# Softmax sums of 16 heads taken from ones in the unused value columns, in place of eight separate matmuls per batch

## The chip, the cores and the metric

The kernel runs on one core of one Trainium2 chip. The metric is the device time of one execution in microseconds (us), lower is better. Engines are TensorE (PE, with its weight loads shown apart as PEld), VectorE (DVE), ScalarE (ACT), GpSimd (POOL) and SyncE (SP), which issues most transfers. All data is fp32.

## What is computed

Four transformer blocks run one after the other on x (16 batches of 128 rows of 256) with a context of the same shape. The change concerns the attention with 16 heads of width 16, which occurs in block 0 (self attention, then cross attention), in block 1 (ten chosen rows of each batch) and in block 3 (cross attention). Cut to what matters:

```python
def _mha(q_in, kv_in, in_w, in_b, out_w, out_b):
    q, k, v = heads(...), heads(...), heads(...)          # (16 batches, 16 heads, 128 rows, 16)
    scores = jnp.einsum('bhqd,bhkd->bhqk', q, k) / jnp.sqrt(jnp.float32(dh))
    attn = jax.nn.softmax(scores, axis=-1)
    out = jnp.einsum('bhqk,bhkd->bhqd', attn, v)
    out = out.transpose(0, 2, 1, 3).reshape(q_in.shape[0], q_in.shape[1], D)
    return out @ out_w.T + out_b

x = x + _mha(_ln(x), _ln(x), ...)          # block 0, first stage
x = x + _mha(_ln(x), _ln(ctx), ...)        # block 0, second stage; then a mixture of 8 experts, 2 per row
x = ... ten rows of each batch replaced by their attention to ctx      # block 1
x = ... grouped attention with 4 key heads and a gated MLP             # block 2, not touched
x = x + _mha(layer_norm(x), ctx, ...)      # block 3
```

## The kernel before, in words

`attention` (L526) is a pipeline over batches, called twice: with two stages (32 batches, block 0, with the router of the experts mixed in from slot 20 on) and with one stage (16 batches, block 3). Each engine runs one Python loop over a slot number t, so what an engine does in slot t stands in the order in which the loop writes it, and semaphores tie the engines together. Where a text speaks of the start of slot t, it is the start of that slot's `scores_turned` (L679). In a slot of the middle:

- PE: `scores(t + 1)` (L669) writes the scores of the next batch to four PSUM banks `scores`; then work for the groups ahead (turns L645, projections L652, value projections L661); `products(t - 1)` (L689 and L694) into PSUM bank 4; more work for the groups ahead; `scores_turned(t)` (L679), which writes the same four banks; a turn of the row maxima (L811); and, in odd slots, `rows_out` (L704), the output projection of two finished batches.
- DVE: the row maxima of batch t + 1 (L1006, two instructions over 128x1024); in even slots the addition of the output rows to x (L1022); the division for batch t - 1 (L1027, L1028); the maxima subtracted in the queries (L1038); statistics of the batch 11 ahead (L983 to L990).
- ACT: copies and projections' biases (L839 to L867), then the exponentials of batch t (L912, two instructions), whose results are the turned probabilities `PT2`.
- POOL: standardizes the rows of the groups of four batches ahead (L944) and adds the output bias to x (L951).

The four banks `scores` are written twice in a slot, so a slot has a loop through three engines: L679 writes them, L912 reads them, L669 writes them, L1006 reads them, and the next L679 may start.

A slot's work ahead depends on its phase, (t + 5) % 4. Phase 0 (t = 3, 7, ...) has two turns of 4 x 128 columns, as has phase 1 in the two stages that attend to the context; phase 1 in the self attention and phase 2 there have one projection of 512 columns ahead of `scores_turned`; phase 2 in the other stages and phase 3 have two pieces of that kind, or a projection and values. The additions L1022 come in phases 1 and 3.

Values are kept padded (`VP`, and `tok_V` in block 1): each head has 32 columns, of which 16 hold its values and 16 hold zeros, values first for even heads and last for odd ones. Two heads thus add up to the 32 rows of bank 4 that belong to r, and four r run in four column tiles of PE. Columns 0 to 255 of bank 4 get the numerators, columns 256 to 511 the sums, from a stationary operand `ones_half` that is one in half its columns. DVE then takes the reciprocal of 128x256 sums and multiplies. Block 1 does the same for groups of four batches in `products` (L1909 on), `divide` (L2151 on) with `tok_` names; its four groups g = 0 to 3 are handled in a loop of their own.

## Time and profile before

| what | value |
|---|---|
| median of 3 runs | 1432.4 us (1427.1 to 1432.89) |
| profiled execution: span from first to last instruction | 1426.0 us |
| profiled execution: PE busy | 1293.6 us, 91% of the span |
| DVE / ACT / POOL busy | 673.4 / 622.1 / 429.4 us |
| first call of `attention` (slots 0 to 31) | about 35 to 340 us of the span |
| block 1 | about 700 to 810 us |
| second call of `attention` (slots 0 to 15) | about 1278 to 1423 us |

The profile describes one execution. What the execution takes outside its span is not in it: the median of the runs is 6.4 us above the span, the lowest run 1.1 us. A row of the timeline gives the start and length of a few merged instructions, the engine, the line, the instruction, and in brackets the idle time ahead with the instruction that ended it. Matmuls in fp32 appear as two records each, so the 16 matmuls of `products` are x32.

### The profile page before, as it was taken

Reading aid. Unit: us, or ns where it says so; the run is one execution under the profiler, and the core shown is the slowest. Engines: PE = TensorE matmul, PEld = TensorE weight load, DVE = VectorE, ACT = ScalarE, POOL = GpSimd, SP = SyncE. Lnnn points to the kernel's source line nnn. Section 1 sums busy time; section 2 is a strip of 40 time slices with the busy share of each in tenths; the row PEclk is TensorE's granted clock in tenths of the full one; section 3 lists DMA queues with packets and bytes.
Section 4 is the critical chain, followed back from the end, with each engine's and each line's share of the span. In section 5 each row is a group of like instructions: output and inputs, shape, how many; then the busy total and the mean of one; then the engine's idle time right before and its main releaser. Section 6 shows DMA issues by size and latency. Waiting matters only on the chain. (4 is left out here: it accounts for less than half of the span.)

```text
span 1426.0 us, 34137 instructions
## 1 busy us (share of the span) xinstructions
PE 1293.6 (91%) x13946; PEld 1054.6 (74%) x13946; DVE 673.4 (47%) x1457; ACT 622.1 (44%) x1444; POOL 429.4 (30%) x549
## 2 busy tenths in 40 slices
PE   4899999976799999999688899999999998859996
PEld 2566666655589999998576678888888887736665
DVE  3676777677322000000654645546446445146666
ACT  2444445521445544444222255545546546135442
POOL 3224446153323222244100143433423423032200
PEclk9999999987799999999666999999999999979998
DMA  9000000000589999996410000000000000000000
GB/s 298 2 2 2 2 2 15 11 17 24 133 291 335 344 344 351 355 352 221 148 32 2 3 1 2 2 1 2 1 2 1 2 2 1 1 1 2 17 17 31
DMA packets 80042, 120.11 MB, mean 84 GB/s; under 512 B 12112, under 2 KB 62544, under 8 KB 79760
## 3 DMA queue, kind: packets, MB, share of 16 engines
q1 hardware_dynamic: 73840, 106.62, 22.4%
q0 software_dynamic: 4768, 10.26, 2.0%
q8 instruction: 112, 1.84, 0.6%
q10 hardware_dynamic: 1280, 1.04, 0.2%
q14 instruction: 42, 0.34, 0.1%
HBM read 108.43 MB, written 9.48 MB: 83 GB/s over the span
## 5 line engine op out<-in xcount | busy, mean ns | idle before, releaser
L1759 ACT ACTIVATE w_ca<-scores,fc1b 128x128 f32<-128x128 f32 x312 | 114.5, 368 | 139.7 <-PE scores L1714 118.6
L912 ACT ACTIVATE reg<-scores 128x1024 f32<-128x1024 f32 x96 | 93.1, 1021 | 160.9 <-PE scores L679 160.7
L1714 PEld LDWEIGHTS scores<-reg 128*128 128x128 f32 x1248 | 146.7, 194 | 6.4 <-issue 2.5
L1714 PE MATMUL scores<-reg 128*128 128x128 f32 x1248 | 147.7, 277 | 3.1 <-issue 1.1
L1724 PE MATMUL bank<-reg,w_ca 128*128 128x256 f32 x624 | 141.1, 379 | 0.3 <-DVE small L1784 0.3
L1006 DVE TENSOR_REDUCE reg<-scores 128x8 f32<-128x1024 f32 x96 | 113.0, 1219 | 54.6 <-PE scores L669 54.5
L2311 ACT ACTIVATE reg<-reg,mx 128x128 f32<-128x128 f32 x256 | 99.1, 389 | 85.1 <-DVE mx L2460 84.8
L2386 POOL TENSOR_TENSOR reg<-reg,rden 128x512 f32<-128x512 f32 x64 | 66.6, 1041 | 212.3 <-DVE rden L2465 212.2
L1793 DVE TENSOR_TENSOR reg<-bank,reg 128x256 f32<-128x256 f32 x39 | 16.6, 425 | 240.9 <-PE bank L1724 232.7
L1724 PEld LDWEIGHTS bank<-reg,w_ca 128*128 128x128 f32 x624 | 115.6, 190 | 14.5 <-DVE small L1784 0.3
L1576 PE MATMUL scores<-reg 128*128 128x128 f32 x1024 | 122.5, 279 | 0.5 <-ACT reg L2327 0.5
L1576 PEld LDWEIGHTS scores<-reg 128*128 128x128 f32 x1024 | 119.8, 196 | 0.7 <-ACT reg L2327 0.7
L2248 PE MATMUL bank<-reg,w_ca 128*128 128x256 f32 x512 | 118.8, 385 | 0.8 <-issue 0.8
L2248 PEld LDWEIGHTS bank<-reg,w_ca 128*128 128x128 f32 x512 | 94.7, 190 | 26.6 <-issue 13.2
L1027 DVE RECIPROCAL reg<-bank 128x256 f32<-128x256 f32 x48 | 84.2, 1754 | 30.6 <-PE bank L694 29.8
L852 ACT ACTIVATE reg<-bank,qk_bias,shape_c 128x512 f32<-128x512 f32 x96 | 69.6, 779 | 59.1 <-PE bank L652 58.8
L1141 POOL DMA_INDIRECT expert_out<-reg,block_ids_of x39 | 39.5, 1012 | 143.1 <-DVE reg L1793 75.0
L2471 DVE TENSOR_TENSOR w_ca<-scores,w_ca 128x512 f32<-128x512 f32 x32 | 22.1, 692 | 109.9 <-PE scores L1576 109.9
L679 PEld LDWEIGHTS scores<-reg 32*128 32x128 f32 x1536 | 48.3, 189 | 31.8 <-issue 31.7
L669 PEld LDWEIGHTS scores<-reg 32*128 32x128 f32 x1536 | 50.0, 193 | 28.7 <-ACT reg L912 20.2
L679 PE MATMUL scores<-reg 32*128 32x128 f32 x1536 | 57.2, 286 | 14.0 <-DVE reg L1006 14.0
L669 PE MATMUL scores<-reg 32*128 32x128 f32 x1536 | 59.5, 291 | 7.8 <-ACT reg L912 5.1
(278 smaller groups left out, 2347.5 us busy)
## 6 DMA issues: line engine op xcount, KB each, us to landing
reg<-in_fc SPq DMA_DIRECT2D x78, 1024.0 KB, 7.4
reg<-expert_out SPq DMA_DIRECT2D x16, 256.0 KB, 3.9
xres<-in_x SPq DMA_DIRECT2D x4, 512.0 KB, 10.6
ctxr<-in_ctx SPq DMA_DIRECT2D x1, 2048.0 KB, 14.8
w_l<-in_w_l SPq DMA_DIRECT2D x2, 1024.0 KB, 12.1
routed_rows<-reg SPq DMA_DIRECT2D x8, 256.0 KB
out<-xres SPq DMA_DIRECT2D x8, 256.0 KB, 2.6
w_sa<-in_w_sa SPq DMA_DIRECT2D x1, 1024.0 KB, 8.5
```

The costliest lines, as they stand in the source:

```text
L669: ins = nc.tensor.matmul(S[r][:, (2 * s + c) * P:(2 * s + c + 1) * P], Qs[rows_of(r), (b // GB) % 2, s, c, batch(b)], Ks[rows_of(r), (b // ...
L679: ins = nc.tensor.matmul(S[r][:, (2 * s + c) * P:(2 * s + c + 1) * P], Ks[rows_of(r), (b // GB) % 2, s, c, batch(b)], Qs[rows_of(r), (b // ...
L852: ins = nc.scalar.activation(dst[:, g % 2, s, m, :], bank[:, :], ACT.Identity, scale=scale[:, s:s + 1], bias=bias[:, s, m:m + 1])
L912: ins = nc.scalar.activation(PT2[:, t % 2, 2 * half:2 * half + 2, :, :, :].rearrange("p r s c q -> p (r s c q)"), scores4[:, 2 * half:2 * ...
L1006: ins = nc.vector.tensor_reduce(mxpad.rearrange("p (c n d) -> p n c d", c=C, d=DH)[:, 4 * half:4 * half + 4, :, 0], scores4[:, 2 * half:2 ...
L1027: link(nc.vector.reciprocal(rd, banks[4][:, 2 * P:4 * P]))
L1576: ins = nc.tensor.matmul(bank[:, k * P:(k + 1) * P], w[:, c, w0:w0 + P], src[:, c, :], start=(c == 0), stop=(c == C - 1))
L1714: ins = nc.tensor.matmul(S[n % 4][:, 0:P], up_w8[j % 2][:, c, f * P:(f + 1) * P], xbT[:, j % 2, c, :], start=(c == 0), stop=(c == C - 1))
L1724: ins = nc.tensor.matmul(T[j % 2][:, 0:D], h1[:, j % 2, f, :], down_w8[j % 2][:, f, :], start=(f == 0), stop=(f == FC - 1))
L1759: nc.scalar.activation(h1[:, j % 2, f, :], S[n % 4][:, 0:P], ACT.Gelu, bias=fc1b[:, bass.ds(e * FC + f, 1)]).then_inc(M["fc1_free"], 1)
L2248: ins = nc.tensor.matmul(bank[:, 0:D], src[:, f, :], w[:, f, :], start=(f == 0), stop=(f == FC - 1))
L2311: ins = nc.scalar.activation(v[:, a, :], v[:, a, :], ACT.Exp, bias=cols_of(mx, n)[:, a:a + 1], accum_out=cols_of(psum, n)[:, a:a + 1])
```

## The change

Values are padded with ones in place of zeros. One matmul of a head then gives 32 rows: 16 of numerators and 16 copies of the head's sum. The heads no longer add up in pairs: even heads go to columns 0 to 255 of bank 4, odd heads to columns 256 to 511, each matmul starting and ending its own accumulation. The eight `ones_half` matmuls of a batch go, and the 16 of `products` stay (in block 1, 64 stay and 8 go per group).

Numerator and sum of a head now stand in different rows. DVE turns bank 4 in blocks of 32x32 (128x512, from PSUM), takes the reciprocal of one of each 16 equal sums (128x16 in all), and turns these, spread over 16 columns each, back into rows (128x256), so that each numerator has its inverse sum beside it. ACT copies the even half of bank 4, with the rows that hold sums scaled to zero; DVE adds the odd half, likewise masked, and multiplies with the inverse sums. A batch has three more DVE instructions and one more ACT instruction, and four fresh waits. PE may overwrite bank 4 when the masked sum is made (`nd_read`), no longer after the multiplication (`o_ok`).

The diff also drops functions that nothing calls (`Jobs`, `dve_softmax`, `pe_products` and others), and four memsets of `ones_half` at the start. Its core:

```diff
+        def inverse_sums(dve, link, turned, out_, sums_read, k):
+
+            nc.vector.transpose(turned, banks[4][:, :]).then_inc(sums_read, 1)
+            dve.wait_ge(sums_read, k)
+            sums_of = turned[:, DH:DH + 2 * (C * P - DH)].rearrange("p (u x) -> p u x", u=2)[:, :, 0:C * P - DH:32]
+            link(nc.vector.reciprocal(den_inv[:, :, :].rearrange("p n u -> p u n"), sums_of))
+            link(nc.vector.transpose(out_.rearrange("p (n u d) -> p n u d", n=8, u=2),
+                                     den_inv[:, :, :].unsqueeze(3).to_broadcast([P, 8, 2, DH])))
...
                     def products(b):
-                        for c in range(C):
-                            for s in range(2):
+                        for odd in range(2):
+                            for c in range(C):
                                 for r in range(4):
-                                    nc.tensor.matmul(banks[4][rows_of(r), c * P:(c + 1) * P],
-                                                     VP[:, (b // GB) % 2, b % GB, 8 * c + 2 * r + 1 - s, :],
-                                                     PT2[:, b % 2, r, s, c, :], start=(s == 0), stop=(s == 1))
-                        for s in range(2):
-                            for r in range(4):
-                                ins = nc.tensor.matmul(banks[4][rows_of(r), C * P:2 * C * P], ones_half[:, s, :],
-                                                       PT2[:, b % 2, r, s, :, :], start=(s == 0), stop=(s == 1))
+                                    a0 = (2 * odd + c) * P
+                                    ins = nc.tensor.matmul(banks[4][rows_of(r), a0:a0 + P],
+                                                           VP[:, (b // GB) % 2, b % GB, 8 * c + 2 * r + odd, :],
+                                                           PT2[:, b % 2, r, 1 - odd, c, :], start=True, stop=True)
                         ins.then_inc(M["nd_full"], 1)
...
                             if t - 1 >= 1:
-                                pe.wait_ge(M["o_ok"], t - 1)
+                                pe.wait_ge(M["nd_read"], t - 1)
...
                         if t < LATE:
                             routed_rows(t)
+                        if 0 <= t - 1 < N:
+                            act.wait_ge(M["sums_read"], t)
+                            if t - 1 >= 1:
+                                act.wait_ge(M["nd_read"], t - 1)
+                            nc.scalar.activation(even_part, banks[4][:, 0:2 * P], ACT.Copy, scale=head_rows[:, 1:2])\
+                                .then_inc(M["num_ok"], 1)
                         if 0 <= t < N:
                             act.wait_ge(M["st_full"], t + 1)
...
                             dve.wait_ge(M["nd_full"], b + 1)
-                            link(nc.vector.reciprocal(rd, banks[4][:, 2 * P:4 * P]))
-                            nc.vector.tensor_tensor(oT_a[:, (b // 2) % 2, :, (b % 2) * P:(b % 2 + 1) * P],
-                                                    banks[4][:, 0:2 * P].rearrange("p (c q) -> p c q", c=C),
-                                                    rd.rearrange("p (c q) -> p c q", c=C), ALU.mult).then_inc(M["o_ok"], 1)
+                            inverse_sums(dve, link, den_turned, rd, M["sums_read"], b + 1)
+                            dve.wait_ge(M["num_ok"], b + 1)
+                            o = oT_a[:, (b // 2) % 2, :, (b % 2) * P:(b % 2 + 1) * P]
+                            nc.vector.scalar_tensor_tensor(out=o, in0=banks[4][:, 2 * P:4 * P].rearrange("p (c q) -> p c q", c=C),
+                                                           scalar=head_rows[:, 0:1], in1=even_part.rearrange("p (c q) -> p c q", c=C),
+                                                           op0=ALU.mult, op1=ALU.add).then_inc(M["nd_read"], 1)
+                            dve.wait_ge(M["nd_read"], b + 1)
+                            nc.vector.tensor_tensor(o, o, rd.rearrange("p (c q) -> p c q", c=C), ALU.mult).then_inc(M["o_ok"], 1)
...
-                            nc.vector.memset(VP[:, 0, :, :, :], 0.0).then_inc(M["pad_ok"], 1)
-                            nc.vector.memset(VP[:, 1, :, :, :], 0.0).then_inc(M["pad_ok"], 1)
+                            nc.vector.memset(VP[:, 0, :, :, :], 1.0).then_inc(M["pad_ok"], 1)
+                            nc.vector.memset(VP[:, 1, :, :, :], 1.0).then_inc(M["pad_ok"], 1)
...
+                def even_heads(g):
+                    act.wait_ge(M["tok_sums_read"], g + 1)
+                    if g > 0:
+                        act.wait_ge(M["tok_nd_read"], g)
+                    nc.scalar.activation(tok_even, banks[4][:, 0:2 * P], ACT.Copy, scale=head_rows[:, 1:2])\
+                        .then_inc(M["tok_num_ok"], 1)
...
+                    even_heads(g)
                     if g + 1 < G:
                         queries(g + 1)
```

Block 1 has the same edits in its `products` and `divide`, with `tok_` names.

PE in slot 4 of block 0's first stage, before: a projection, `products`, the eight matmuls with `ones_half`, then `scores_turned`.

```order
L652 MATMUL bank<-reg,w_sa 128x512 [waits b_free,a_free,sub_ok]
L652 MATMUL bank<-reg,w_sa 128x512
L689 MATMUL bank<-reg 32x128 [waits o_ok,p_ok]
L689 MATMUL bank<-reg 32x128 x15
L694 MATMUL bank<-reg,ones_half 32x256 x8
L679 MATMUL scores<-reg 128x128 [waits max_ok,sub_ok]
L679 MATMUL scores<-reg 128x128 x15
```

The same place after the change:

```order
L474 MATMUL bank<-reg,w_sa 128x512 [waits b_free,a_free,sub_ok]
L474 MATMUL bank<-reg,w_sa 128x512
L512 MATMUL bank<-reg 32x128 [waits nd_read,p_ok]
L512 MATMUL bank<-reg 32x128 x15
L501 MATMUL scores<-reg 128x128 [waits max_ok,sub_ok]
L501 MATMUL scores<-reg 128x128 x15
```

The row with `ones_half` is gone, and `products` waits for `nd_read` in place of `o_ok`; nothing else on PE moves.

DVE in slot 4, before, from the maxima to the subtraction:

```order
L1006 TENSOR_REDUCE reg<-scores 128x4x2 [waits s_full]
L1006 TENSOR_REDUCE reg<-scores 128x4x2
L1022 TENSOR_TENSOR xres<-bank,xres 128x512 [waits biased,c_full]
L1027 RECIPROCAL reg<-bank 128x256 [waits nd_full]
L1028 TENSOR_TENSOR reg<-bank,reg 128x2x128 [waits chain]
L1038 SCALAR_TENSOR_TENSOR reg<-bank,shape_c,reg 128x2x128 [waits mt_full]
```

And after:

```order
L831 TENSOR_REDUCE reg<-scores 128x4x2 [waits s_full]
L831 TENSOR_REDUCE reg<-scores 128x4x2
L847 TENSOR_TENSOR xres<-bank,xres 128x512 [waits biased,c_full]
L341 STREAM_TRANSPOSE reg<-bank 128x512 [waits nd_full]
L344 RECIPROCAL den_inv<-reg 128x2x8 [waits sums_read]
L345 STREAM_TRANSPOSE reg<-den_inv 128x256 [waits chain]
L855 SCALAR_TENSOR_TENSOR reg<-bank,shape_c,reg 128x2x128 [waits num_ok,chain]
L859 TENSOR_TENSOR reg<-reg 128x2x128 [waits nd_read]
L867 SCALAR_TENSOR_TENSOR reg<-bank,shape_c,reg 128x2x128 [waits mt_full]
```

Five instructions, each waiting for the one ahead of it or for ACT, stand where two stood.

ACT in slot 4, before: the biases of a projection, then the exponentials.

```order
L839 ACTIVATE reg<-bank,cols 128x512 [waits b_full]
L852 ACTIVATE reg<-bank,qk_bias,shape_c 128x512 [waits a_full]
L852 ACTIVATE reg<-bank,qk_bias,shape_c 128x512
L912 ACTIVATE reg<-scores 128x1024 [waits st_full]
L912 ACTIVATE reg<-scores 128x1024
```

And after:

```order
L658 ACTIVATE reg<-bank,cols 128x512 [waits b_full]
L671 ACTIVATE reg<-bank,qk_bias,shape_c 128x512 [waits a_full]
L671 ACTIVATE reg<-bank,qk_bias,shape_c 128x512
L732 ACTIVATE reg<-bank,shape_c 128x256 [waits nd_read,sums_read]
L737 ACTIVATE reg<-scores 128x1024 [waits st_full]
L737 ACTIVATE reg<-scores 128x1024
```

The copy of the even heads (L732) stands in ACT's queue ahead of the exponentials, and waits for DVE's first block turn (`sums_read`).

## Rows read from the trace of the kernel before

**Rows 1.** The page: busy time of the engines over the span.

```profile
PE 1293.6 (91%) x13946; PEld 1054.6 (74%) x13946; DVE 673.4 (47%) x1457; ACT 622.1 (44%) x1444; POOL 429.4 (30%) x549
```

**Rows 2.** Waits of PE, whole span: engine, line, waited for; us in total, times, longest.

```profile
PE scores L679 <- DVE reg L1006: 14.0, 10, 3.4
```

**Rows 3.** Timeline of slot 4, block 0: start us, us, engine, line.

```profile
76.15 1.98 PE L652 MATMUL bank<-reg,w_sa 128*128 128x512 f32 x4
76.29 2.36 DVE L1006 TENSOR_REDUCE reg<-scores 128x8 f32<-128x1024 f32 x2 [1.37 <-PE scores L669]
...
78.07 1.08 PE L689 MATMUL bank<-reg 128*32 128x128 f32 x32
...
78.56 0.68 DVE L1022 TENSOR_TENSOR xres<-bank,xres 128x512 f32<-128x512 f32 x1
...
78.97 1.05 PE L694 MATMUL bank<-reg,ones_half 128*32 128x256 f32 x16
...
79.94 1.17 PE L679 MATMUL scores<-reg 32*128 32x128 f32 x32
80.08 1.76 DVE L1027 RECIPROCAL reg<-bank 128x256 f32<-128x256 f32 x1 [0.83 <-PE bank L694]
...
81.18 1.94 ACT L912 ACTIVATE reg<-scores 128x1024 f32<-128x1024 f32 x2 [1.56 <-PE scores L679]
```

**Rows 4.** Timeline of slot 12, block 3 (no work ahead left).

```profile
1384.65 1.17 PE L679 MATMUL scores<-reg 32*128 32x128 f32 x32 [0.69 <-DVE reg L1006]
...
1391.38 0.68 DVE L1022 TENSOR_TENSOR xres<-bank,xres 128x512 f32<-128x512 f32 x1
1391.61 1.17 PE L679 MATMUL scores<-reg 32*128 32x128 f32 x32 [0.70 <-DVE reg L1006]
...
1392.84 1.94 ACT L912 ACTIVATE reg<-scores 128x1024 f32<-128x1024 f32 x2 [5.03 <-PE scores L679]
```

**Rows 5.** Timeline: starts of slots 2, 3, 11 and 12, block 0.

```profile
64.34 1.17 PE L679 MATMUL scores<-reg 32*128 32x128 f32 x32
...
71.82 1.17 PE L679 MATMUL scores<-reg 32*128 32x128 f32 x32
...
143.03 1.17 PE L679 MATMUL scores<-reg 32*128 32x128 f32 x32
...
150.42 1.17 PE L679 MATMUL scores<-reg 32*128 32x128 f32 x32
```

**Rows 6.** Timeline of slots 9 and 10, block 0, where DVE waits for POOL.

```profile
125.63 4.85 POOL L944 TENSOR_SCALAR reg<-ctxr,mv,rstd 128x256 f32<-128x256 f32 x4
...
130.57 0.43 DVE L983 BATCH_NORM_STATS2 st<-xres 128x6 f32<-128x256 f32 x1 [5.59 <-issue]
...
133.99 1.17 PE L679 MATMUL scores<-reg 32*128 32x128 f32 x32 [2.04 <-DVE reg L1006]
...
135.37 3.58 PE L661 MATMUL bank<-w_sa,reg 128*128 128x256 f32 x8
```

**Rows 7.** Timeline of group 0, block 1.

```profile
720.61 1.91 PE L1926 MATMUL bank<-w_sa,ones_half 128*32 128x256 f32 x16
...
725.02 1.10 PE L1934 MATMUL bank<-w_l,reg 128*128 128x256 f32 x4 [1.41 <-DVE reg L2154]
```

**Rows 8.** Groups of instructions by line and form: busy us, mean ns, idle before.

```profile
L1027 DVE RECIPROCAL reg<-bank 128x256 f32<-128x256 f32 x48 | 84.2, 1754 | 30.6 <-PE bank L694 29.8
...
L694 PE MATMUL bank<-reg,ones_half 128*32 128x256 f32 x768 | 51.6, 387 | 0.0
...
L1038 DVE SCALAR_TENSOR_TENSOR reg<-bank,shape_c,reg 128x256 f32<-128x256 f32 x96 | 41.8, 477 | 25.8 <-PE bank L811 22.0 <-remote 3.7
...
L1022 DVE TENSOR_TENSOR xres<-bank,xres 128x512 f32<-128x512 f32 x24 | 16.4, 683 | 4.5 <-PE bank L704 4.4
...
L2465 DVE RECIPROCAL rden<-psum 128x4 f32<-128x4 f32 x64 | 11.2, 175 | 7.7 <-ACT reg L2311 6.9
...
L2327 ACT ACTIVATE reg<-scores 128x256 f32<-128x256 f32 x16 | 6.1, 381 | 10.0 <-PE scores L2255 10.0
```

More of the change, by code:

```diff
@@ L50 @@
 ROWS = ["sa_ob", "ca_ob", "l1_ob", "l3_ob", "l1_sw"]
-class Jobs:
-    def __init__(self, names):
-        self.at = {n: (k % 2, k // 2) for k, n in enumerate(names)}
-        assert len(self.at) == len(names)
-    def __getitem__(self, name):
-        return self.at[name]
 def build(nc, A, out):
@@ L358, in pe_turn_rows @@
-        def pe_turn_rows(pe, J, names, src, ok):
-            for c in range(C):
-                bank = claim(pe, J, names[c])
-                for j in range(GB):
-                    if c == 0 and ok is not None:
-                        pe.wait_ge(ok, j + 1)
-                    ins = nc.tensor.transpose(bank[:, j * P:(j + 1) * P], src[:, j, c * P:(c + 1) * P], ident[:])
-                ins.then_inc(q_full[J[names[c]][0]], 1)
-        def act_affine(act, J, names, dst, gain, bias):
-            for c in range(C):
-                bank = await_full(act, J, names[c])
-                if gain is None:
-                    ins = nc.scalar.activation(dst[:, c, :], bank[:, :], ACT.Copy)
-                else:
-                    ins = nc.scalar.activation(dst[:, c, :], bank[:, :], ACT.Identity, scale=col(gain, c),
-                                               bias=col(bias, c) if bias else 0.0)
-                ins.then_inc(q_free[J[names[c]][0]], 1)
@@ L495, in act_products @@
-        def act_products(act, J, name, bv, dst_cols):
-            bank = await_full(act, J, name)
-            for c in range(C):
-                ins = nc.scalar.activation(oT[:, c, dst_cols], bank[:, c * P:(c + 1) * P], ACT.Identity, bias=col(bv, c))
-            ins.then_inc(q_free[J[name][0]], 1)
         class Home:
```

155 lines of the change are left out of this document (23 added, 132 removed).

## The prediction, made before the changed kernel ran

> **What bounds the kernel now.** I read the page's busy shares first, then who PE waits for, then the timeline of single slots, which decides. PE is busy for 91% of the span [rows 1], and its largest wait inside the two calls of `attention` is for the maxima, 14.0 us in ten waits [rows 2]. So these 48 slots are mostly a queue of PE work; but the loop through three engines lies close under it, and the price of anything taken off PE must be read against that loop.
>
> Slot 4 shows both [rows 3]. From `scores_turned` to the exponentials is 81.18 - 79.94 = 1.24 us, and they take 1.94; the next scores begin right behind, so this part of a slot is always about 3.23. The other part runs from L669 to the next L679. PE's queue fills it here: L652 at 76.15, `products` at 78.07, the sums at 78.97, L679 at 79.94. DVE's maxima began at 76.29 and ended by 78.56, 1.4 us before L679 started. Slot 12 of block 3 has no work ahead, and there the maxima end last: PE idles 0.70 before L679, and the slot takes 1391.61 - 1384.65 = 6.96 us [rows 4]. That is the floor, with or without the sums. Slots of phase 0 take 71.82 - 64.34 = 7.48, those of phase 1 with context 150.42 - 143.03 = 7.39 [rows 5]: they can lose 0.5 and no more.
>
> **What goes from PE.** Eight matmuls of 256 columns per batch, 51.6 us of busy time in 48 batches [rows 8], 1.05 us each with overlaps. What the queue gains is the distance: from the start of the sums to L679 is 79.94 - 78.97 = 0.97, and from the end of `products` (79.15) to that of the sums (80.02) 0.87 [rows 3]. I take 0.90. The 16 matmuls that stay have the same form; only their targets and flags change.
>
> **What DVE gets.** Before: reciprocal and product, 80.08 to 82.29 by slot 4's pattern, of which 1.754 is the reciprocal [rows 8] and about 0.42 the product. After: a block turn of 128x512 from PSUM, a reciprocal of 128x16, a block turn of 128x256, the masked sum, the product. The reciprocal costs (1754 - 175) / 252 = 6.27 ns per element by its two sizes [rows 8], so 16 elements cost 175 + 12 x 6.27 = 250 ns. The masked sum is the form of L1038, 0.48 us; the product as before, 0.42. No block turn is in this trace. Its lower bound is the plain pass over 128x512 from PSUM, 0.683 us (L1022), its upper bound the reciprocal's rate, 6.27 ns per element: 3.3 us, and 1.7 for the 256. I take 0.68 and 0.42, the pass, because a turn moves each element once and computes nothing, as L1022 nearly does. The sum is 0.68 + 0.25 + 0.42 + 0.48 + 0.42 = 2.25 us. Two instructions with no wait between them overlap by 0.09: the maxima last until 76.29 + 2.36 = 78.65, and L1022 starts at 78.56 [rows 3]. A wait costs that overlap and, I estimate, some 0.03 more. With three more waits DVE's part is about 2.3 instead of 2.15 from its start to that of the subtraction: 0.15 us longer per slot. DVE is at 47% [rows 1], but where it ends a slot, this counts.
>
> The Trainium skill (VectorE: DVE Perf Modes, section Rules for kernel authors) speaks against this change: for chained DVE operations it says to minimize the number of operations. By that rule five in place of two are a loss. In the rows the fixed share of an instruction is small against the reciprocal: even with three more instructions the sum is only 0.15 longer, so the rule changes nothing in the working beyond that. For the block turn, the Trainium skill (Vector Engine (DVE) Microarchitecture Reference, section The reshape front-end and per-opcode configuration) states one element per cycle and lane; no run here shows it yet, and with it the sum would be the one I use.
>
> **What ACT gets, and who waits.** The even half is 128x256 from PSUM: 0.381 us as L2327 [rows 8]. It stands ahead of the exponentials in ACT's queue and waits for the first block turn, which waits for `nd_full` and stands on DVE behind the maxima and, in even slots, behind L1022. So a second path leads to the exponentials: maxima end, L1022 (0.60), block turn (0.06 + 0.70), copy (0.05 + 0.38 + 0.05). From the end of the maxima this is 1.24 us without and 1.84 with L1022; the path over L679 is 0.14 + 1.24 = 1.38 (L679 starts 0.23 after L1022, which starts 0.09 before the maxima end) [rows 4]. Hence in slots where the maxima end last, an even slot's exponentials now come 0.46 later than L679 alone would let them; in phase 1 with context this eats the gain of 0.4 down to 0.1, since the exponentials could start no earlier than 0.1 before where they do now. `nd_read` comes several us before the next `products`, and `o_ok` a slot before its `rows_out`; both are covered by the slot itself.
>
> **The 48 slots**, by what ends last after the change:
> - PE's queue, with long work behind `products` or ahead of it (slots 1, 2, 5, 6, 21, 22, 25, 26 of block 0; 1, 2, 5, 6, 9, 10 of block 3): 14 x 0.90 = 12.6 us.
> - Phase 1 of the self attention and slots 23 and 24: in slot 4 the copy would end at 79.15 + 0.06 + 0.70 + 0.48 = 80.39, against 81.18 now: 4 x 0.8 = 3.2.
> - Phase 0 (five slots of block 0, two of block 3): down to the floor, 7 x 0.45 = 3.2.
> - Phase 1 with context: 5 x 0.1 = 0.5.
> - Three pairs, slots 9/10, 13/14 and 17/18. POOL standardizes until about 130.5, DVE's statistics wait for it for 5.59 us, the maxima stand behind them, and PE idles 2.04 [rows 6]. Those chains start from DVE statistics two slots earlier and hold no PE work, so nothing is gained, and DVE's longer part (0.15) and the copy behind L1022 (0.3) are lost: 3 x -0.45 = -1.4.
> - Slots 27 to 31 of block 0 (the router's work on DVE) and 11 to 15 of block 3: held by the maxima, even slots lose 0.3: -1.6.
> - Tails: the last `products`, divisions and projections, where PE, DVE and PE follow each other: +0.5 and +1.2.
> - The two first slots: nothing.
>
> Sum 12.6 + 3.2 + 3.2 + 0.5 - 1.4 - 1.6 + 1.7 = 18.2 us.
>
> **Block 1.** The four groups run at the lower clock (1.91 us for the sums) and `products`, division, L1934 follow each other directly: PE idles 1.41 before L1934 [rows 7]. Of 1.9 saved, the longer division takes 0.5 (0.15, and ACT's copy and queue): 3 x 1.3, and 0.5 in the last group, where the clock is up and other matmuls stand between: 4.4 us. Nothing else changes: the memsets write ones at the cost of zeros, the four POOL memsets at the start lie under the first loads.
>
> **Total** 22.6 us off the span of 1426.0. The median of the runs lies 6.4 above the span, the lowest 1.1; I set the saving against the median: 1432.4 - 22.6 = 1409.8.
>
> **Rivals.**
> - *The block turn takes twice a pass* (1.22 us for 512 elements, 0.68 for 256), for fp32 moved in two halves. Then the path over the copy is 0.54 longer. Twelve of the slots with long work do not see it; two and the four of the second group lose 0.54 each, seven of phase 0 0.42, five of phase 1 0.54, the pairs 1.3, ten at the ends 0.5, tails and block 1 0.8 six times: 3.2 + 2.9 + 2.7 + 3.9 + 5 + 4.8 = 22.5. That eats all: 1432. For it: nothing in the trace shows a turn. Against it: a pass needs no second read. 0.10.
> - *The clock.* PE idled 2.04 before slot 10, and the L661 behind it took 3.58 us where others take 1.9: 1.7 lost [rows 6]. The change makes idle time of what it saves: about 1.2 to 1.8 in slots 14 and 18, which have none now. Should the granted clock fall there too, and in two to four slots near the ends, 3.4 to 10 us go: 1413 to 1420. 0.14.
> - *The maxima are no floor*: if DVE picks up faster or the L679 queue moves up everywhere, 48 x 0.97 + 7 - 2 = 51, 1381. The 0.70 of idle time in rows 4 speaks against it. 0.04.
> - *Slower*: the block turn at half the reciprocal's rate, 3.4 ns per element: 1.75 and 0.88 us. The path over the copy grows by 1.07 and DVE's part by 1.5. Then the short slots lose 1.0 to 1.5 each: some 6 x 1.07 + 12 x 1.0 + 3 x 2.6 + 10 x 1.07 + 6 x 1.5 = 46, and the time is 1432.4 + 23 = 1456. It decides from about 2.4 ns per element, where the gain is nil. Nothing but the lack of a row speaks for it. 0.06.
> - The forecast, 1399 to 1418, has 0.66.
>
> **How the numbers follow.** Low end: 0.97 in place of 0.90 in 18 slots (1.3 more), floor slots losing 0.5 (0.3), block 1 at the full 1.9 each (3.2), and runs as near their span as the lowest one (5.3 below the median): 1399.7, so 1399. High end: the clock at its worst (1420) or turns half as dear again as a pass (half of 22.5 lost, 1421), and 3 for the runs' spread: 1424. A measurement of this kernel can tell about 0.5% from no change, 7 us. Faster by more than that: 0.66 + 0.14 + 0.04 = 0.84; within it 0.10; slower 0.06.
>
> **What would show it.** The page after should have PE busy about 55 us less (51.6 and block 1's 6.0, less some). Block turns in the groups of instructions at 0.68 and 0.42 us; the floor slots at 6.96 to 7.1; slot 4 at 7.3; the pairs unchanged at 20.1 to 20.3 us; PE's waits for the maxima up from 14 us to some 20. In the copy's row, idle time ended by the block turn. I am wrong if the turns cost over 1 us, if ACT's wait for them holds back the exponentials in slots of long work too, or if slots fall under 6.9.

## The result, and the profile after

| | before | after |
|---|---|---|
| median of the runs | 1432.41 us (1427.1 to 1432.89) | 1418.49 us (1415.44 to 1418.86) |
| ratio, 95% interval | | 0.990, 0.9876 to 0.9924 |
| span of the profiled execution | 1426.0 us | 1416.9 us |
| start of slot 0 to start of slot 27, block 0 | 246.49 us | 241.53 us |
| slot 27 to slot 31, block 0 | 37.37 us | 43.84 us |
| block 1, start to the first scores of block 2 | 117.2 us | 116.7 us |
| block 2, untouched by the change, to slot 0 of block 3 | 475.8 us | 473.1 us |
| slot 0 to slot 15, block 3 | 125.53 us | 119.93 us |

The kernel became 13.9 us faster, where 22.6 were forecast. The two profiled executions differ by 9.1 us only: that of before is one of its faster ones (its runs in all comparisons reach from 1423.8 to 1439.3 us), that of after lies at its median. Not all of the 9.1 is the change's, either: 2.7 us of it lie in block 2, whose code is the same (471.4 to 479.7 us in the other twelve profiled executions). One of the four executions of experiment nine's kernel was in a slower state of the chip (1575.9 us, granted clock 0.81) and is left out.

Page of after: busy time of the engines, the line that answers to [rows 1]. PE lost 29.6 us of busy time and not 55: what it lost in matmuls it partly gave back in slower ones. In slots 28 to 31, with fewer matmuls, it is busy for 35.8 us and not 29.1 (granted clock 0.62, 0.82 before), and in block 1 it is busy as long as before, 95.4 and 95.2 us (0.66, 0.71 before).

```profile
PE 1264.0 (89%) x13114; PEld 1044.7 (74%) x13114; DVE 681.5 (48%) x1613; ACT 644.4 (45%) x1496; POOL 430.3 (30%) x545
```

Groups of after by line and form (busy us, mean ns, idle before), which answer to [rows 2, 8]: PE's matmuls of `scores_turned` (L501), then the division on DVE (block turn L341, reciprocal L344, second block turn L345, masked sum L855, product L859) and ACT's copy of the even half (L732).

```profile
L501 PE MATMUL scores<-reg 32*128 32x128 f32 x1536 | 64.3, 308 | 32.6 <-DVE reg L831 31.6 <-issue 1.0
...
L341 DVE STREAM_TRANSPOSE reg<-bank 128x512 f32<-128x512 f32 x48 | 34.1, 711 | 11.2 <-PE bank L512 9.6 <-remote 1.4
L855 DVE SCALAR_TENSOR_TENSOR reg<-bank,shape_c,reg 128x256 f32<-128x256 f32 x48 | 23.2, 484 | 4.8 <-ACT reg L732 3.2
L345 DVE STREAM_TRANSPOSE reg<-den_inv 128x256 f32<-128x256 f32 x52 | 23.2, 445 | 1.8
L732 ACT ACTIVATE reg<-bank,shape_c 128x256 f32<-128x256 f32 x48 | 22.8, 474 | 104.3 <-DVE reg L341 104.3
L859 DVE TENSOR_TENSOR reg<-reg 128x256 f32<-128x256 f32 x48 | 22.1, 461 | 1.7
...
L344 DVE RECIPROCAL den_inv<-reg 128x16 f32<-128x16 f32 x48 | 12.2, 254 | 1.6
```

The division is 0.711 + 0.254 + 0.445 + 0.484 + 0.461 = 2.36 us, where 2.25 was worked out: each part came out 0.004 to 0.04 dearer. But the wait of PE for the maxima rose from 14.0 to 31.6 us and not to 20, and the mean of the L501 matmuls from 286 to 308 ns: stretches at the lower clock that were not there before. The timeline of slots 9 and 10 of after shows both; it answers to [rows 6].

```profile
119.23 4.85 POOL L769 TENSOR_SCALAR reg<-ctxr,mv,rstd 128x256 f32<-128x256 f32 x4
...
124.17 0.43 DVE L808 BATCH_NORM_STATS2 st<-xres 128x6 f32<-128x256 f32 x1 [6.66 <-issue]
...
127.59 2.09 PE L501 MATMUL scores<-reg 32*128 32x128 f32 x32 [4.25 <-DVE reg L831]
129.61 0.69 PE L630 MATMUL bank<-ident,reg 128*128 128x128 f32 x2
130.09 3.57 PE L483 MATMUL bank<-w_sa,reg 128*128 128x256 f32 x8
```

By the kernel's semaphores, DVE's statistics of a group's first batch (L808) write a buffer that POOL reads until the end of its standardization (the trace names no releaser, but they start 0.09 us after it), and the maxima stand behind them. PE came to the wait sooner, so it waited 4.25 us instead of 2.04, and the scores behind took 2.09 us instead of 1.17: slot 10 takes 13.51 us (12.16 before) and slot 11 9.75 (9.04). The hold has a length of its own: from POOL's first instruction for the group to the start of slot 10, 14 or 18 it is 16.11 us in all three places before, and 16.36 to 16.40 after. Before, PE's own queue was just as long in slots 14 and 18, so that it showed no wait there; after, it waits. Slot 18 before, then after:

```profile
203.52 1.99 PE L661 MATMUL bank<-w_ca,reg 128*128 128x256 f32 x8
205.45 1.17 PE L679 MATMUL scores<-reg 32*128 32x128 f32 x32
```

```profile
197.19 0.43 DVE L808 BATCH_NORM_STATS2 st<-xres 128x6 f32<-128x256 f32 x1 [5.72 <-issue]
...
200.62 1.17 PE L501 MATMUL scores<-reg 32*128 32x128 f32 x32 [2.35 <-DVE reg L831]
```

### The profile page after: what moved, and what is told of

Read it like the earlier page. It is cut to its first block and busy times, and to the rows that moved or that the text cites. A ratio compares the mean times of both kernels' runs of the same rounds, so it can differ in the third digit from the quotient of the medians.

```text
span 1416.9 us, 32778 instructions
## 1 busy us (share of the span) xinstructions
PE 1264.0 (89%) x13114; PEld 1044.7 (74%) x13114; DVE 681.5 (48%) x1613; ACT 644.4 (45%) x1496; POOL 430.3 (30%) x545
## 5 line engine op out<-in xcount | busy, mean ns | idle before, releaser
L501 PE MATMUL scores<-reg 32*128 32x128 f32 x1536 | 64.3, 308 | 32.6 <-DVE reg L831 31.6
L501 PEld LDWEIGHTS scores<-reg 32*128 32x128 f32 x1536 | 54.9, 208 | 48.8 <-issue 48.7
L491 PEld LDWEIGHTS scores<-reg 32*128 32x128 f32 x1536 | 50.0, 192 | 29.8 <-ACT reg L737 21.4
L732 ACT ACTIVATE reg<-bank,shape_c 128x256 f32<-128x256 f32 x48 | 22.8, 474 | 104.3 <-DVE reg L341 104.3
L491 PE MATMUL scores<-reg 32*128 32x128 f32 x1536 | 59.7, 290 | 8.8 <-ACT reg L737 6.6
```

What stands on the lines that cost most here:

```text
L491: ins = nc.tensor.matmul(S[r][:, (2 * s + c) * P:(2 * s + c + 1) * P], Qs[rows_of(r), (b // GB) % 2, s, c, batch(b)], Ks[rows_of(r), (b // ...
L501: ins = nc.tensor.matmul(S[r][:, (2 * s + c) * P:(2 * s + c + 1) * P], Ks[rows_of(r), (b // GB) % 2, s, c, batch(b)], Qs[rows_of(r), (b // ...
```

## The experiments

Each ran against the kernel before, in four comparisons; with that of the result they are five, in which the median of before moved between 1431.2 and 1434.6 us. So two experiments of different comparisons are held against each other by their ratios; their medians alone can be off by 3 us. Slot lengths are of one profiled execution each. "Slot n" is the time from the start of that slot's `scores_turned` back to that of the slot before it.

### The two halves of the change apart

**One.** In the kernel before, the sums' matmuls are taken out, in every batch but the first of each call and in block 1, and nothing else. The division then works on old sums: this kernel leaves out what makes its result right, and only its time is of use.

```diff
-                        for s in range(2):
-                            for r in range(4):
-                                ins = nc.tensor.matmul(banks[4][rows_of(r), C * P:2 * C * P], ones_half[:, s, :],
+                        if b == 0:
+                            for s in range(2):
+                                for r in range(4):
+                                    ins = nc.tensor.matmul(banks[4][rows_of(r), C * P:2 * C * P], ones_half[:, s, :],
```

> The kernel before, with its eight matmuls on ones_half left out in every batch but the first of each call, and in block 1 altogether, so that the division works on old sums; DVE and ACT do exactly what they did. This is what PE gains, alone. Theory A (the clock): block 0 gets ahead by some 6 to 8 us until slot 27, then PE's longer idle time there lets the granted clock fall, and block 0 ends within 3 us of the kernel before; the whole is 10 to 16 us faster, 1417 to 1422. Theory B (the longer division and ACT's wait take the gain back): here they are absent, so block 0 ends 12 us or more earlier, and the whole is 22 us or more faster, at most 1410.

Measured: 1415.27 us, ratio 0.987 (0.983 to 0.991). Neither theory's total came: it is 2 us under A and 5 above B. From slot 2 to slot 9 every slot has the length of after (8 and 9 at 7.25 and 7.26 us), so there the longer division costs nothing. From slot 10 up to slot 27 it costs 3.9 us: slot 10 is 12.99 instead of 13.51, 13, 17 and 21 9.17 instead of 9.41, 14 and 18 11.31 instead of 11.64 and 11.60, 23 8.50 instead of 8.98, and 19, by the clock, 7.33 instead of 8.62. But slot 10 is longer than before's 12.16 with less work on PE: the wait for POOL gives the gain back, whoever made it. Slots 28 to 31 took 48.6 us here, with neither the longer division nor the copy, against 43.8 in after.

**Two.** The kernel after, with the sums' matmuls put back as idle ones of the same size, in block 1 too.

```diff
                     def products(b):
+                        for s in range(2):
+                            for r in range(4):
+                                nc.tensor.matmul(banks[4][rows_of(r), C * P:2 * C * P], VP[:, (b // GB) % 2, b % GB, s, :],
+                                                 PT2[:, b % 2, r, s, :, :], start=True, stop=True)
```

> The changed kernel, with eight matmuls of 256 columns added to PE ahead of products in every batch and group, whose result products overwrites: PE does as much as before, DVE and ACT do the new division. This is what the new division costs, alone. Theory A: little, 0 to 4 us over the kernel before, 1432 to 1437, since the block turns cost a pass. Theory B: 8 to 14 us over it, 1440 to 1446.

Measured: 1446.44 us, ratio 1.009 (1.006 to 1.012): 14 us above before, the top of Theory B, where PE's part alone brings 17. The two don't add up to the change's 13.9, and neither is a price that holds elsewhere: with PE's part out, the division costs 3 us (1418.49 against 1415.27, intervals that overlap). Slots 1 to 9 are those of before to 0.01 us, slots 10, 14, 15, 18 and 19 are 0.22 to 0.26 longer, slot 26 1.57; up to slot 27 that is 3.0 us. Slots 28 to 31 take 50.3 us, 12.9 more than before, and block 1 121.4. Under a full PE queue the division is hidden, in the waits it is not. The slots 28 to 31 are more than half of the 23.1 us between the two profiled spans, and executions differ there for another reason (below), so the 14 us are not shown to be the division's.

### The clock

**Three.** The kernel after, with the same idle matmuls in slots 10, 14, 18 and 27 to 31 alone.

```diff
                     def products(b):
+                        if router is not None and b + 1 in (10, 14, 18, 27, 28, 29, 30, 31):
+                            (the eight matmuls of the experiment above)
```

> The changed kernel, with the same eight idle matmuls only in slots 10, 14, 18 and 27 to 31 of block 0, where the maxima end last and PE waits. Theory A: PE's idle stretches are 1 us shorter, the granted clock stays up in slots 28 to 31, and the kernel is 3 to 7 us faster than the changed one, though it does more work: 1411 to 1415. Theory B: PE waits there anyway, so the time is that of the changed kernel, 1416 to 1420.

Measured: 1417.99 us, ratio 0.991 (0.988 to 0.993): the same as after, as Theory B had it; Theory A's gain didn't come. The idle matmuls lie ahead of the wait for the maxima and not in it; PE still idles there (3.38 us in slot 10, 4.25 in after). Windows of after (first) and of this kernel over slots 11 and 19: stretch, its length, busy time of PE, PEld, DVE, ACT and POOL, granted clock, share of the DMA engines and GB/s.

```profile
127.50:137.00 9.50, 9.37 (x114) 7.31 (x114) 6.64 (x14) 4.28 (x6) 0.00 (x0) 0.68 0.00 0
...
200.90:210.00 9.10, 8.71 (x139) 6.93 (x138) 7.95 (x20) 4.42 (x7) 0.00 (x0) 0.81 0.01 3
```

```profile
127.50:137.00 9.50, 9.12 (x113) 7.25 (x114) 6.60 (x15) 4.28 (x6) 0.00 (x0) 0.66 0.01 2
...
200.90:210.00 9.10, 8.09 (x149) 6.66 (x150) 8.82 (x22) 4.76 (x8) 0.00 (x0) 1.00 0.01 3
```

In slot 19 the clock was kept (1.00 for 0.81), and the slot fell from 8.62 to 7.59 us: that is the price of the lower clock in that slot, 1.0 us. In slot 11 it wasn't, and the slot stayed at 9.8. And it fell elsewhere instead: slot 24 has 0.82, and takes 9.65 us where it took 8.06 in after.

### The hold by POOL

**Four.** The kernel after, with the statistics of a group's first batch issued one slot later, behind that slot's maxima. Then POOL has ended when DVE comes to them.

```diff
-                        if t + AHEAD < N:
-                            row_stats(t + AHEAD)
+                        for n in (t - 1 + AHEAD, t + AHEAD):
+                            if 0 <= n < N and (n % GB == 0) == (n < t + AHEAD):
+                                row_stats(n)
```

> The changed kernel, with the statistics of a group's first batch, which wait for POOL, moved one slot later on DVE, so that the maxima of slots 10, 14 and 18 no longer stand behind them. Theory A: those three slots fall from 13.5, 11.6 and 11.6 us to 9.4 each and PE has no idle time there, so that the clock stays up behind them too: 8 to 12 us faster than the changed kernel, 1407 to 1411. Theory B: the same three slots shrink, but nothing behind them changes: 6 to 8 us, 1411 to 1413.

Measured: 1406.13 us, ratio 0.983 (0.980 to 0.987), 12.4 us under after by the medians, 9.5 by the ratios; just under Theory A's 1407 to 1411. Timeline of slots 9 and 10:

```profile
119.37 4.85 POOL L769 TENSOR_SCALAR reg<-ctxr,mv,rstd 128x256 f32<-128x256 f32 x4
...
123.42 1.17 PE L501 MATMUL scores<-reg 32*128 32x128 f32 x32
...
125.79 0.42 DVE L808 BATCH_NORM_STATS2 st<-xres 128x6 f32<-128x256 f32 x1
```

POOL works as before, DVE's statistics come 1.57 us after its end and wait no more, PE doesn't idle, and its scores run at the full clock (1.17 us). Slots 10, 11, 14, 15, 18, 19 and 23 take 9.20, 7.06, 9.18, 7.06, 9.18, 7.35 and 8.86 us, against 13.51, 9.75, 11.64, 7.29, 11.60, 8.62 and 8.98: 13.5 us less.

**Five.** The same edit on the kernel before, as a control.

> The kernel before, with the statistics of a group's first batch moved one slot later; the control of the same edit on the kernel after, which gained 12.4 us there (slots 10, 11, 14 and 18 fell from 13.51, 9.75, 11.64 and 11.61 us to 9.20, 7.06, 9.18 and 9.19). Theory C, the hold: in the kernel before the same hold shows in slots 10 and 11 alone (12.16 and 9.04 us, where 10.05 and 7.48 stand in block 3; slots 14 and 18 are at 10.06 already), so this kernel gains about 2.1 + 1.6 = 3.7 us: 1427 to 1430, and with the hold out of both the change is worth 1428.5 - 1406 = 22 us, its forecast. Rival D, the edit frees the same in both: 1418 to 1422, and the hold says nothing of why the change fell short.

Measured: 1429.77 us, ratio 0.9971 (0.9949 to 0.9993). Up to slot 27 it is 3.68 us ahead of before, all of it in slots 10 and 11 (12.16 to 10.05 and 9.04 to 7.47). So the hold costs before 3.7 us and after 13.5: **9.8 us of the change's gain are spent there.** With the hold out of both, the change is worth 0.9834 / 0.9971 = 0.9863 by the ratios, 19.6 us, give or take 6 (1429.77 - 1406.13 = 23.6 by the medians, of two comparisons). That lies near the 22.6 of the forecast, but not for the forecast's reasons: it had the hold in it. By its own 0.90 for each of the six slots of the pairs, and without the 1.4 that it took off for them, it would have said some 29 for kernels without the hold.

### The price of the division on its path

**Six.** The kernel after, with ACT's copy of the even half done by DVE, in block 1 too.

```diff
-                            nc.scalar.activation(even_part, banks[4][:, 0:2 * P], ACT.Copy, scale=head_rows[:, 1:2])\
-                                .then_inc(M["num_ok"], 1)
+                            nc.vector.tensor_scalar(even_part, banks[4][:, 0:2 * P], head_rows[:, 1:2], None, ALU.mult)\
+                                .then_inc(M["num_ok"], 1)
```

> The kernel after, with the copy of the even half (numerators times the even head's mask) done by VectorE just ahead of the masked sum, instead of by ScalarE beside the reciprocal and the second block turn. ScalarE loses 0.474 us for each batch and group, VectorE takes about 0.45. If ScalarE's copy is hidden and VectorE's chain sets the slots over 7.06 us (Theory C: the division's length behind the hold), then only those slots grow: some 20 of 64 by 0.2 to 0.45 us, and each of 16 groups of block 1 by up to 0.45: 1424 to 1432. If ScalarE's copy pushes back the exponentials on which the products wait (Theory B), the kernel gains 0.2 to 0.4 us in the slots that wait for the exponentials: 1408 to 1415.

Measured: 1425.1 us, ratio 0.9933 (0.991 to 0.9957). Theory C's range holds it. Slots 10, 14 and 18 grow to 14.01, 12.15 and 12.14, by 0.50, 0.51 and 0.54: behind the hold DVE's length counts whole. Slots 13, 17 and 21 shrink from 9.41 to 9.16: there ACT's copy does hold back the exponentials, by 0.24, as Theory B had it for such slots. Slots at 6.97 and 7.06 stay. Where the clock fell, slots move by more: slot 15 takes 8.62 us instead of 7.29 (granted clock 0.80, 1.00 in after) and slot 24 9.65 instead of 8.06 (0.82). Here and in the next expectation the text counts 64 batches and 16 groups; there are 48 and 4, as the x52 of L345 shows.

**Seven.** The kernel after, with the second block turn issued twice.

```diff
+            link(nc.vector.transpose(out_.rearrange("p (n u d) -> p n u d", n=8, u=2),
+                                     den_inv[:, :, :].unsqueeze(3).to_broadcast([P, 8, 2, DH])))
```

> The kernel after, with the second block turn (the one that spreads the inverse sums over their rows, 0.445 us) issued twice for every batch and group; the second writes the same values again. It is the price of VectorE's time in the division. Theory C: VectorE's chain sets only the slots behind a hold and those of long VectorE work; so slots at 6.97, 7.06 and 7.25 us stay, slots 10, 14 and 18 grow by 0.4 to 0.5, slots 13, 17, 21 by up to 0.4, block 1's 16 groups by 0 to 0.4: 1424 to 1432. Theory B, the division sets every slot: 64 batches and 16 groups at 0.445 make 30 us: 1440 to 1450.

Measured: 1431.47 us, ratio 0.9997 (0.997 to 1.0025): 13 us for 0.445 us of DVE time in each of 48 batches and 4 groups (23 us in all; Theory B with the right count says 1442), the whole of the change's gain. Slots 1 to 9, 11 to 13 and 20 to 22 stay within 0.11; slots 10, 14 and 18 grow by 0.48 each; slots 23 to 26, where DVE has the router's work, by 0.24, 1.66, 0.63 and 2.27. Two of these are far above 0.445, and both ran at a lower granted clock (0.82 in slot 24, 0.79 in slot 26; 1.00 in both in after). So DVE's time is a price only where DVE is what a slot waits for, and there it can cost more than its own length, by the clock of the slot behind.

### Slots 28 to 31

Here after took 43.84 us and before 37.37 between the starts of slots 27 and 31: 6.5 us lost, more than the 5.0 us that the change had brought from slot 0 to slot 27. Timeline of after from the start of slot 27: POOL's indirect writes (L1112), and ACT, DVE and PE, which start late with no releaser that the trace can name ("remote"), or stop in mid-batch ("issue").

```profile
282.85 1.24 POOL L1112 DMA_INDIRECT sorted_ids<-token_ids,pick_row  x1 [0.19 <-issue]
284.11 2.09 PE L501 MATMUL scores<-reg 32*128 32x128 f32 x32 [3.24 <-DVE reg L831]
...
288.60 1.94 ACT L737 ACTIVATE reg<-scores 128x1024 f32<-128x1024 f32 x2 [3.51 <-remote]
...
290.01 0.88 DVE L867 SCALAR_TENSOR_TENSOR reg<-bank,shape_c,reg 128x256 f32<-128x256 f32 x2 [3.68 <-remote]
...
291.98 0.96 POOL L1112 DMA_INDIRECT sorted_ids<-token_ids,pick_row  x1 [0.30 <-issue]
292.12 0.26 PE L491 MATMUL scores<-reg 32*128 32x128 f32 x1 [0.34 <-issue]
...
294.25 0.81 PE L491 MATMUL scores<-reg 32*128 32x128 f32 x4 [0.93 <-issue]
```

**Eight and nine.** All indirect writes issued behind the last slot, in the kernel after and in the kernel before.

```diff
-                        for k in routed_sets("place", t):
-                            router.scatter(pool, k)
                     if router is not None:
+                        for k in range(len(router.sets)):
+                            router.scatter(pool, k)
```

> The kernel after, with all 32 of GpSimd's indirect writes of the routing table issued behind the last slot of block 0, instead of in bursts of four and eight in slots 24 to 31 (nothing is left out). All 32 at 1.27 us are 40 us, of which 25 to 40 come on top of the time at the end of block 0. What is read is slots 28 to 31 (start of slot 27 to start of slot 31: 37.4 us before, 43.8 after). Theory E, instructions: TensorE stops in mid-batch there with no wait shown (pieces of 1 and 3 matmuls of a batch of 32 with pauses of 0.45 to 0.93 us), and ScalarE and VectorE start 3.5 us late (marked remote), always beside a burst; the engines' instructions arrive late while the indirect writes run. With no burst there: no such pause over 1 us, 34 to 38 us from slot 27 to slot 31, and the same in the kernel before with the same edit. Rival A, the granted clock: the clock still falls to 0.5 to 0.8 there, 41 to 44 us. Total 1435 to 1455 by E, 1443 to 1460 by A.

> The kernel before, with all 32 indirect writes of the routing table issued behind the last slot of block 0, as in the same edit of the kernel after. Theory E (instructions late beside the bursts): 34 to 38 us from slot 27 to slot 31 as in the other, no pause over 1 us without a wait, and the difference between the two kernels with this edit is 5 to 7 us larger than the 13.9 us between the two as they stand: 18 to 22 us. Rival A (the clock alone, lost by the kernel after and kept by the kernel before): 37 us here and 41 to 44 there, difference 13 to 15 us.

Measured: 1434.87 us with the change (ratio 1.0004) and 1450.66 without (1.0106). From slot 27 to slot 31 it is 34.77 and 33.89 us, and no engine stops without a named releaser:

```profile
283.08 2.09 PE L501 MATMUL scores<-reg 32*128 32x128 f32 x32 [3.24 <-DVE reg L831]
...
285.23 1.94 ACT L737 ACTIVATE reg<-scores 128x1024 f32<-128x1024 f32 x2 [1.17 <-PE scores L501]
285.83 0.88 DVE L867 SCALAR_TENSOR_TENSOR reg<-bank,shape_c,reg 128x256 f32<-128x256 f32 x2 [0.53 <-PE bank L630]
...
288.11 1.17 PE L491 MATMUL scores<-reg 32*128 32x128 f32 x32
```

So without the bursts the stops are gone from these slots; slots 28 to 31 are 3.5 us shorter than in before's execution and 9.1 shorter than in after's, and the change itself loses 0.9 there. A burst alone doesn't make a stop at once, though: in before's execution eight writes run beside slot 28, from 288.70 us, and it takes 7.45 us with none; DVE's 3.69 us "remote" and PE's pause of 1.47 come in slot 29. And the difference between the two kernels is 15.8 us here (14.6 by the ratios), not the 18 to 22 expected: the medians don't show the 6.5 us. Experiment five suggests why: it has before's code in these slots and took 42.72 us (slot 28: 13.88 instead of 7.45). So before's profiled execution seems to have been lucky there; two executions are all that speak for it.

**Ten and eleven.** Idle matmuls of 16 columns ahead of the first batch's products, 32 or 64 of them (the same edit, `n` 32 or 64), to move TensorE's later instructions to other places in its program.

```diff
                     def products(b):
+                        if router is not None and b == 0:
+                            for k in range(n // 4):
+                                for r in range(4):
+                                    nc.tensor.matmul(banks[4][rows_of(r), C * P:C * P + 16], VP[:, 0, 0, 0, :],
+                                                     PT2[:, 0, r, 0, 0, 0:16], start=True, stop=True)
```

> The kernel after, with 32 idle matmuls of 16 columns ahead of the first batch's products in block 0 (about 1 us, once), whose result is overwritten. They move every later instruction of TensorE by 64 places in its program and nothing else. Theory E: slots 28 to 31 take 43.8 us in the kernel after and 37.4 before because there the engines' instructions arrive late beside the bursts of indirect writes, and where a load of instructions falls depends on the place in the program; so the time from slot 27 to slot 31 changes by over 2 us (between 35 and 48) while all other slots of block 0 stay within 0.1. Rival A, the granted clock: slots 27 to 31 stay at 43 to 45 us. Total 1410 to 1424 by E, 1418 to 1421 by A.

> The kernel after, with 64 such idle matmuls in the same place (about 2 us, once): 128 places. Theory E: slots 27 to 31 take another time than in the kernel after and than with 64 places, between 35 and 48 us, by over 2 us for at least one of the two. Rival A: 43 to 45 us in both.

Measured: 1418.64 and 1418.22 us (ratios 0.9901 and 0.9908); slots 28 to 31 take 44.84 and 44.00 us, slot 28 13.58 and 13.54, as Rival A had it. So moving TensorE's program to these two places changed nothing, and this form of the theory fell. But ScalarE and VectorE are the first to start late (at 288.60 and 290.01, TensorE stops at 292.12), and their programs were not moved; that form wasn't tried. Why the engines stop beside the bursts stays open.

**Twelve.** Experiment four, and each set's writes cut so that four follow each other, the rest going with the next set.

```diff
-                for b in range(b0, b0 + n):
-                    for s in range(2):
+                self.left = (self.left if k else []) + [(b, s) for b in range(b0, b0 + n) for s in range(2)]
+                for b, s in [self.left.pop(0) for _ in range(4 if k + 1 < len(self.sets) else len(self.left))]:
```

> The kernel after with the statistics moved (1406 us), and in addition no burst of the indirect writes longer than four until the last: of the first set's eight, four go with it and four with the next set, every set passes four on, and the last issues eight. Theory E', the long burst: the stop of ScalarE, VectorE and TensorE in slot 28 (13.56 us there, 8.9 with the writes held to the end) comes only while eight writes run one behind the other. Then slot 28 falls to 8 to 10 us and slots 28 to 31 from 43.7 to 36 to 40 us; the last burst may cost 5 us ahead of the expert stage: 1401 to 1408. Rival: any burst does it, from its third microsecond on: slot 28 stays over 12 us and the whole at 1405 to 1411.

Measured: 1404.54 us (1402.7 to 1407.62), ratio 0.980 (0.975 to 0.985). Slot 28 falls from 13.56 to 10.41 us, slots 28 to 31 from 43.73 to 40.10, between what the two theories gave. ACT's late start is still there (3.57 us idle ahead of it in slot 28), so a burst of four does it too. The whole isn't told apart from experiment four; both beat the two kernels.

## Why the prediction was right, and where it was too high

The direction held, and so did most of the working, but not the size: 1418.5 lies half a microsecond above the likeliest case (1399 to 1418, held at 0.66) and inside what the rival of the clock gave (1413 to 1420, held at 0.14). By stages of the two profiled executions, forecast against measured: up to slot 27 of block 0 about 11.5 us against 5.0; slots 28 to 31 less than 1.6 lost against 6.5 lost; block 1 4.4 against 0.5; block 3 up to slot 15 about 6 against 5.6. Outside these, 0.9 ahead of slot 0 and 2.7 in block 2 came besides. In the order of the prediction's steps:

- **The loop and the floor held.** Slots of phase 0 are at 7.06 us, those of phase 1 with context at 6.97, slot 4 at 7.25 (7.3 forecast). Phase 1 with context came out better than forecast, 5 x 0.42 = 2.1 us instead of 0.5: the copy isn't late there as worked out.
- **PE's queue, 14 slots at 0.90 = 12.6 us: measured 12.6, with some luck.** Eight of them gave 0.85 to 0.87 and five 0.59 to 0.72. In three of the five the copy holds back the exponentials by 0.24 (experiment six), which was one of the prediction's own signs of being wrong. And slot 2 of block 3 gave 2.49, of which 1.6 isn't the change's: that slot takes 9.18 to 9.19 or 10.80 to 10.83 us in executions of kernels with it. Without these 1.6 the term is 11.0.
- **The division on DVE: 0.24 us longer, where 0.15 was forecast** (2.37 us from its start to the subtraction in slots without a wait, 2.13 before). The Trainium skill (Vector Engine (DVE) Microarchitecture Reference, section The reshape front-end and per-opcode configuration) gives one element per cycle and lane for the block turn; the trace agrees, 711 ns for 512 elements, where the plain pass over as many takes 683. ACT's copy took 474 ns and not 381: L2327, from which it was taken, carries no per-partition scale from a tile; whether that is the reason wasn't tried.
- **The pairs behind POOL, and the slots behind them: 4.0 us too much.** The prediction kept the pairs at -1.4 us and let slots 11, 15 and 19 gain 1.35. That nothing is gained in a pair was right, and the price was near for the first: the three pairs lost 0.50, 0.95 and 0.92 us. The larger error is behind them: slots 11, 15 and 19 lost 1.68 together (9.75 instead of 9.04, 7.29 instead of 7.47, 8.62 instead of 7.47), with the granted clock at 0.68 in slot 11 (0.81 before) and 0.81 in slot 19 (1.00 before), behind PE's longer idle time in slots 10 and 18. The prediction knew that PE would idle in slots 14 and 18, and wrote so under the rival of the clock, but its sum has no term for it. Experiments four and five give another number, what the hold costs the change against kernels without it: 9.8 us. It is not the error of the forecast, which had never counted on a gain there.
- **The clock**, held at 0.14 as a rival of its own, is thus a part of what happened: slot 19 pays 1.0 us for it (experiment three). It shows again in block 3, where PE's scores in slot 13 take 2.09 us, slot 14 takes 8.88 us instead of 6.97, and slots 11 to 15 lose 2.4; and in block 1.
- **Slots 23 and 24** were to gain 1.6 and lost 1.06, all of it in slot 23. There DVE's statistics for the router wait for POOL too, 3.10 us (0.52 before), and the maxima stand behind them: a second hold, of the same kind. Experiment one, without the longer division, has 8.50 us in slot 23, against 7.91 before and 8.98 after; so more than half of the loss is the hold's.

```profile
240.35 0.75 DVE L996 BATCH_NORM_STATS2 small<-xres 128x6 f32<-128x256 f32 x2 [3.10 <-POOL reg L1017]
...
243.77 1.17 PE L501 MATMUL scores<-reg 32*128 32x128 f32 x32 [1.86 <-DVE reg L831]
```

- **Slots 28 to 31**, forecast at less than 1.6 lost, lost 6.5 in this pair of executions. With the indirect writes out of them the change loses 0.9. Of the 6.5, 5.4 would be the luck of before's execution, if 42.72 us (experiment five, the same code) is the usual length and not 37.37. The prediction had no term for it and took before's slots as their usual lengths.
- **Block 1, forecast 4.4 us: 0.5 in this pair.** Other pairs with the same edit on both sides gave 4.2 (experiments five and four) and 5.8 (nine and eight). In three executions with before's block 1 it took 116.6, 117.2 and 122.6 us, in seven with after's 112.3 to 116.9, mean 114.4. That fits the forecast, but with such spreads it doesn't show it.
- **Against the median.** The saving was set against before's median, 6.4 us above the execution that was costed. That was sound: the saving is 13.9 us in the medians and 9.1 in the spans.

The rivals: a turn at twice a pass and one at half the reciprocal's rate are out by the 711 ns, and the maxima are the floor, as the slots at 6.97 show. The rival of the clock gave the right total, in part by luck: it counted on a fall behind slots 14 and 18 and in two to four slots near the ends. The clock fell behind slot 18, in slots 28 to 31 and in block 3, but not behind slot 14; and the stops beside the indirect writes were no part of it.

## What to carry to other kernels

When work is taken from the engine that bounds a loop, look at every wait that is timed by an engine outside it. A chain that runs at its own pace (here POOL's standardization of 13 us per group) acts as a wall. What is saved beside it is lost (16.1 us before, 16.4 after), and it appears in slots that did not wait before. Then look at the slot behind, which may run at a lower clock. Ask whether the instruction that waits for the chain can stand one slot later; that edit brought 3.7 us to the old kernel and 13.5 to the new one in the slots concerned, nearly as much as the change itself. And an experiment should be paired (the same edit on both kernels), since one stage of a single profiled execution can be off by 5 us.

## What the hardware showed that was not expected

- Beside GpSimd's indirect writes (one each 1.27 us), ScalarE and VectorE stood idle for 3.5 to 3.7 us in after's execution with no releaser in the trace, and TensorE stopped in mid-batch for up to 0.93 us (1.47 in before's). With the writes elsewhere, the same slots took 34 to 35 us; with the writes in them, 37 to 50 us in the twelve other executions.
- DVE's block turn of 32-bit values costs about what a plain pass does: 711 ns for 128x512 from PSUM (683 for the addition L1022 over as many), 445 ns for 128x256 from a broadcast source in SBUF.
- After 4.25 us of idle time TensorE's scores took 2.09 us instead of 1.17, and the granted clock of the 9.5 us that follow was 0.68; the batches at 2.09 ran at the lower level, 1.2 GHz.
